# A LoRA feed-forward kernel: order of the second wave of tile products, waits per chunk ahead of gate, and the last step's transfers

## The chip, the cores and the metric

The kernel runs on one core of a Trainium2 chip, in one launch. The metric is the device time in microseconds. In a profile the engines are PE (TensorE; PEld are its weight loads, which overlap its products), DVE (VectorE), ACT (ScalarE), POOL (GpSimd) and SP (SyncE, which here only issues DMAs). ACT issues DMAs too.

## The reference, cut to what matters

There are 128 sequences of 32 tokens with 512 features, so 4096 tokens. Each sequence b has an adapter id for layer 0 (ids0, 16 adapters) and one for layer 1 (ids1, 64 adapters), each of rank 16.

```python
def lora_add(base, inp, A, B):          # A, B: the sequence's own adapter
    t = einsum('bri,bni->bnr', A[ids0], inp)
    return base + einsum('bor,bnr->bno', B[ids0], t) * 0.5
gate = lora_add(x @ W_gate.T, x, A_gate, B_gate)        # 512 -> 1376
up   = lora_add(x @ W_up.T,   x, A_up,   B_up)
act  = silu(gate) * up
down = lora_add(act @ W_down.T, act, A_down, B_down)    # 1376 -> 512
x1   = x + down @ sign(weight0).T + bias0
c    = einsum('bnr,bor->bno', einsum('bni,bri->bnr', x1, B1[ids1]), A1[ids1])
out  = x1 + c @ (W1 + 2 * sum_n w_n B_n A_n).T + bias1
```

The kernel folds the two square layers into the weights and into tables of rows per adapter in a prologue (sign(weight0) into W_down and B_down, the W1 sum into A1), so each token tile needs gate, up, down and a few small products of rank 16.

## The kernel before, in words

A step g handles 128 tokens, that is four sequences of 32 tokens; there are 32 steps. The first three and the last are written out, and steps 3 to 30 are a loop on each engine. The features of gate and up are cut in three chunks, 0 (352 wide), 1 and 2 (512 wide each), which have their own accumulator banks (`GU_BANK`). Full-precision weights are held as a rounded part and a remainder, so that each product is three rounded ones (`THREE`).

TensorE's step (`step` of the tensor block) is: gate and up of chunks 0, 1 and 2, each 12 products; in the middle of up of chunk 1 a small section (`small`) of narrow products, which gives t, the rank-16 values of the adapters, for this step's gate and up, the previous step's down and, two steps back, layer 1; then the tile session; and last down of the previous step (33 products, `down`). Before `small` it waits (`small_ready`) for the adapters' rows, the three landed chunks of act and the turned x1.

The tile session uses the array as 16 tiles of 32x32: a row group per kind of adapter rows (0 gate, 1 up, 2 layer 1, 3 down) and a column group per sequence b. A product there is in fp32 and shows as two passes, each with a load. The first wave (`first_rows`) has four products per sequence, in the order layer 1 (512 wide), down (512 wide), gate and up of chunk 0 (352 wide). The second wave (`second_rows`) has four per sequence, each 512 wide: row groups 0 and 1 for chunk 1, and row groups 2 and 3, which hold a copy of the same t, for chunk 2. It goes sequence by sequence, row groups 0 to 3 in each. In step 0 the first wave has only row groups 0 and 1, in step 1 row groups 3, 0 and 1.

After the session ACT takes silu of each chunk (L439), DVE multiplies it with up (`gated`, L591; it counts `act_done`) and turns it in blocks of 32 (L595). The turned chunk is sent from SBUF to SBUF by four DMAs (`send_act`), chunks 0 and 1 from ACT's queue and chunk 2 from SP's. Then ACT and DVE split the landed chunk into the two rounded parts for down (L428, L573). Gate of the next step writes the banks that `gated` reads, so it waits for `act_done`: once, ahead of chunk 0, for all three chunks.

SP issues its DMAs in order, in each step: xT and adapter rows of the next step, layer 1's rows (`load_b1`) and x of the previous step (`load_x`), the store of two steps back, sb rows (`load_sbd`, four DMAs), chunk 2, c rows (`load_c`, four DMAs) and the next step's B rows. After the last step, `finish` issues layer 1's rows again (`b1_end`), the last c rows, the last x and two stores. POOL adds bias0 to x when it has landed (L393); DVE then adds the down result (L668 in `finish`). On TensorE `finish` ends with a chain: turn x1 through PSUM (L949), small products for layer 1 (L833), scale and turn on DVE, last rows (L861), last add (L677), store. `keep_busy` (L920) puts products without use into its gaps.

Of the kernel before, what the change touches and what calls it, by code (L numbers as in the profile page):

```python
# [16 lines left out]
GB = P // SEQ  # L17
KC = H // P
CHUNKS = [(1024, 352), (0, 512), (512, 512)]
# [5 lines left out]
NC = len(CHUNKS)  # L25
# [11 lines left out]
PAIR = CHUNKS[0][1] + CHUNKS[1][1]  # L37
ROW = 3 * 512
LINE = 512
GU_BANK = [(4, 5), (0, 1), (2, 3)]  # L40
# [36 lines left out]
def build_adaln_ffn(nc, xT, x, wgu, signT, wd, bd, btab, atab, la, lbw, w1T, a1, b1tab, b1end,  # L77
                    bias, ids, consts, sb_table, c_table, out):
    ctx = ExitStack()
    with ctx:  # L80
# [4 lines left out]
        def place(name, shape, dtype, at=None, line=LINE):  # L85
            n = 4 * int(np.prod(shape[1:]))
            n = (n + line - 1) // line * line
            if at is None:
                at = cursor
            t = nc.alloc_sbuf_tensor_at(name, shape, dtype, offset=at[0])  # L90
            at[0] += n
            return t
# [15 lines left out]
        lhs_sb = place("lhs_sb", [P, P], f32)  # L108
        lhs2_sb = place("lhs2_sb", [P, P], f32)
        loop_at = [cursor[0]]  # L110
        b_rows = place("b_rows", [P, GB, PAIR], f32)
# [54 lines left out]
        def bank(name):  # L166
            return ctx.enter_context(nc.psum_tensor(name, [P, 512], f32))

        gu_ps = [bank(f"gu{n}_ps") for n in range(6)]
# [6 lines left out]
        def sem(name):  # L176
            return ctx.enter_context(nc.semaphore(name))
# [7 lines left out]
        S = {n: sem("pro_" + n) for n in names}  # L185
# [11 lines left out]
        L = {n: sem(n) for n in names}  # L197
# [4 lines left out]
        def after(engine, semaphore, count):  # L202

            if not isinstance(count, int) or count > 0:
                engine.wait_ge(semaphore, count)
# [4 lines left out]
        def first(g):  # L210

            return isinstance(g, int) and g == 0

        def last(g):

            return isinstance(g, int) and g == G - 1
# [13 lines left out]
        def act_in(c):  # L230

            return L[("act_in0", "act_in1", "act_in2")[c]]

        def group(r):

            return slice(r * QUAD, (r + 1) * QUAD)

        def even_rows(r0, r1):

            return slice(r0 * QUAD, r1 * QUAD, 2)  # L240

        def tokens(b):

            return slice(b * SEQ, (b + 1) * SEQ)

        def send(engine, to, tile, w, signal, quarters):
            for q in quarters:
                engine.dma_start(to[:, q * w // 4:(q + 1) * w // 4], tile[q * QUAD:(q + 1) * QUAD, 0:w]
                                 ).then_inc(signal, 16)

        def send_act(engine, g, c, quarters=range(4)):
            engine.wait_ge(L["act_turned"], g * NC + c + 1)
            send(engine, landed[c], act_sb[c], TURN_W[c], act_in(c), quarters)
# [12 lines left out]
        def _(sp):  # L266
# [26 lines left out]
            def row_of(ids, g, b, count):  # L293
                return nc.values_load(idx_feat[0:1, ids, bass.ds(g * GB + b, 1)], engines=[mybir.EngineType.SP],  # L294
                                      min_val=0, max_val=(count - 1) * P,
                                      skip_runtime_bounds_check_because="the ids are clamped on the chip")

            def load_a(g):
                for b in range(GB):
                    at = row_of(0, g, b, R0)  # L300
                    sp.dma_start(a_raw[:, b, :], atab[bass.ds(at, P), :]).then_inc(L["a_in"], 16)
# [8 lines left out]
            def load_b1(g):  # L310
                if last(g + 1 if isinstance(g, int) else g):
                    sp.wait_ge(L["small_mm"], g + 2)
                for b in range(GB):
                    at = row_of(1, g, b, R1)
                    sp.dma_start(b1_raw[:, b, :], b1tab[bass.ds(at, P), :]).then_inc(L["b1_in"], 16)

            def load_sbd(g):
                if isinstance(g, int) and g == 1:
                    sp.wait_ge(L["first_mm"], g + 1)
                for b in range(GB):  # L320
                    at = row_of(0, g, b, R0)
                    sp.dma_start(cs_rows[even_rows(3, 4), b, :], sb_view[bass.ds(at, P), :].rearrange("(r e) w -> r (e w)", e=8)  # L322
                                 ).then_inc(L["sbd_in"], 16)

            def load_c(g, to=2, signal=L["c_in"]):
                for b in range(GB):
                    at = row_of(1, g, b, R1)
                    sp.dma_start(cs_rows[even_rows(to, to + 1), b, :], c_view[bass.ds(at, P), :].rearrange("(r e) w -> r (e w)", e=8)  # L328
                                 ).then_inc(signal, 16)
# [6 lines left out]
            def load_xT(g):  # L336
                sp.wait_ge(L["ad_moved"], g)
                sp.dma_start(xT_raw[:], xT[bass.ds(g * P, P), :].rearrange("p (k t) -> p k t", k=KC)
                             ).then_inc(L["xT_in"], 16)

            def load_x(g):
                if last(g):
                    sp.wait_ge(L["x1_done"], g)
                sp.dma_start(x_in[:], x[bass.ds(g * P, P), :]).then_inc(L["x_in"], 16)

            def store(g):
                sp.wait_ge(L["out_done"], g + 1)
                sp.dma_start(out[bass.ds(g * P, P), :], out_sb[:]).then_inc(L["stored"], 16)

            def step(g, prev, pp, nxt):  # L350
                if nxt is not None:
                    load_xT(nxt)
                    load_a(nxt)
                if prev is not None:
                    load_b1(prev)
                    load_x(prev)
                if pp is not None:
                    store(pp)
                load_sbd(g)
                send_act(sp, g, 2)  # L360
                if prev is not None:
                    load_c(prev)
                if nxt is not None:
                    load_b(nxt)

            def finish(g):
                for b in range(GB):
                    at = row_of(1, g, b, R1)
                    sp.dma_start(b1_end[:, b, 0:KC * RANK], b1end[bass.ds(at, P), :]).then_inc(E["b1_in"], 16)
                load_c(g, 1, E["c_in"])  # L370
                load_x(g)
                store(g - 1)
                sp.wait_ge(L["out_done"], g + 1)
                sp.dma_start(out[g * P:(g + 1) * P, :], x1_turn[:]).then_inc(L["stored"], 16)
                sp.wait_ge(L["stored"], 16 * G)
# [7 lines left out]
            with sp.Fori(3, G - 1) as g:  # L383
                step(g, g - 1, g - 2, g + 1)
            step(G - 1, G - 2, G - 3, None)
            finish(G - 1)


# [37 lines left out]
        def _(act):  # L426
# [42 lines left out]
            def step(g, prev, pp, nxt):  # L469
                if prev is None:  # L470
                    split_up(2, range(KC))
                move_ad(g)
                copy_lhs(g)
                if nxt is not None:
                    split_xT(nxt)
                for c in range(NC):
                    silu(g, c)
                send_act(act, g, 0)
                send_act(act, g, 1)
                split_actT(g, 0)  # L480
                split_actT(g, 1)
                if prev is not None:
                    send_x1(act, prev)
                split_actT(g, 2)
# [279 lines left out]
        def _(pe):  # L764
# [8 lines left out]

            def gate(g, c, pieces=range(KC)):
                f, w = CHUNKS[c]
                if 0 in pieces and c == 0:
                    if first(g):
                        pe.wait_ge(S["wg_lo"], KC)
                    pe.wait_ge(L["xT_lo"], g + 1)
                    after(pe, L["act_done"], g * NC)  # L780
                product(gu_ps[GU_BANK[c][0]][:, 0:w], [(xT_sb[:, k, a, :], wg_sb[:, b, k, f:f + w])
                                                       for k in pieces for a, b in THREE], None,
                        start=0 in pieces, stop=KC - 1 in pieces)
# [103 lines left out]
                last.then_inc(L["first_mm"], 1)  # L887

            def second_rows():
                for b in range(GB):  # L890
                    for r in range(4):
                        c, u = 1 + r // 2, r % 2
                        lhs = lhs_sb if c == 1 else lhs2_sb
                        last = nc.tensor.matmul(gu_ps[GU_BANK[c][u]][tokens(b), :], lhs[group(r), tokens(b)],  # L894
                                                b_rows[group(r), b, CHUNKS[0][1]:PAIR], start=False, stop=True,
                                                skip_group_check=True)
                last.then_inc(L["second_mm"], 1)

            def step(g, prev, pp):
# [197 lines left out]
```

## Time and profile before

| what | value |
|---|---|
| median of 3 runs | 929.75 us (928.69 to 931.73) |
| profiled execution | 930.34 us |
| its span | 928.5 us |
| PE busy | 911.3 us (98%), 10518 products |
| PEld busy | 724.4 us (78%) |
| DVE busy | 413.7 us (45%) |
| ACT busy | 201.3 us (22%) |
| POOL busy | 105.0 us (11%) |
| mean granted clock of TensorE | 0.995 |

The span runs from the first to the last instruction, and all times in rows count from its start. The loop steps are those from about 124 to 880 us. Ends of products are modelled, so a busy PE needn't be PE at its peak; starts are recorded.

### The profile page before, as it was taken

Reading aid. Unit: us, or ns where it says so; the run is one execution under the profiler, and the core shown is the slowest. Engines: PE = TensorE matmul, PEld = TensorE weight load, DVE = VectorE, ACT = ScalarE, POOL = GpSimd, SP = SyncE. Lnnn points to the kernel's source line nnn. Section 1 sums busy time; section 2 is a strip of 40 time slices with the busy share of each in tenths; the row PEclk is TensorE's granted clock in tenths of the full one; section 3 lists DMA queues with packets and bytes.
Section 4 is the critical chain, followed back from the end, with each engine's and each line's share of the span. In section 5 each row is a group of like instructions: output and inputs, shape, how many; then the busy total and the mean of one; then the engine's idle time right before and its main releaser. Section 6 shows DMA issues by size and latency. Waiting matters only on the chain.

```text
span 928.5 us, 27750 instructions
## 1 busy us (share of the span) xinstructions
PE 911.3 (98%) x10518; PEld 724.4 (78%) x10518; DVE 413.7 (45%) x1021; ACT 201.3 (22%) x349; POOL 105.0 (11%) x81
## 2 busy tenths in 40 slices
PE   8998999999999999999999999999999999999996
PEld 5887777777887777778877777788777777887764
DVE  5753344444344444443444444434444444344442
ACT  5742211212112112121121121211211212112110
POOL 0210111010111110101111101011111010111111
PEclk9999999999999999999999999999999999999998
DMA  9924455554554455545544555555444544554432
GB/s 339 411 84 135 111 134 138 148 138 133 145 142 134 130 141 146 139 137 140 142 134 131 140 146 139 133 144 142 133 131 140 146 139 131 145 142 134 132 96 60
DMA packets 146838, 134.69 MB, mean 145 GB/s; under 512 B 53248, under 2 KB 118528, under 8 KB 146688
## 3 DMA queue, kind: packets, MB, share of 16 engines
q1 hardware_dynamic: 91152, 108.42, 40.4%
q10 hardware_dynamic: 54720, 22.83, 9.6%
q0 software_dynamic: 944, 3.15, 0.9%
q8 instruction: 14, 0.23, 0.1%
q14 instruction: 8, 0.07, 0.0%
HBM read 92.11 MB, written 11.01 MB: 111 GB/s over the span
## 4 chain that ended last, share of the span: by engine, by line
PE 94%; SPq 2%; DMA 1%; issue 1%; DVE 1%; POOL 0%; ACT 0%; DVEq 0%
PE gu_ps L768 54%; PE y_ps L803 25%; PE gu_ps L894 4%; PE out_ps L823 3%; PE out_ps L861 2%; PE out_ps L812 1%; PE y_ps L768 1%; PE out_ps L768 1%; PE out_ps L833 1%; PE gu_ps L885 1%; DMA a_raw<-in_a 1%; SPq L328 1%; SPq L294 0%; PE gu_ps L920 0%; SPq L322 0%
## 5 line engine op out<-in xcount | busy, mean ns | idle before, releaser
L768 PE MATMUL gu_ps<-wu_sb,xT_sb 128*128 128x512 f32 (+1 forms) x1152 | 260.8, 371 | 0.0
L768 PE MATMUL gu_ps<-wg_sb,xT_sb 128*128 128x512 f32 (+1 forms) x1152 | 251.8, 367 | 2.8 <-DVE act_sb L591 2.8
L803 PE MATMUL y_ps<-down_sb,actT_sb 128*128 128x512 f32 x1023 | 241.1, 393 | 0.0
L803 PEld LDWEIGHTS y_ps<-down_sb,actT_sb 128*128 128x128 f32 x1023 | 189.6, 188 | 64.4 <-issue 26.0
L768 PEld LDWEIGHTS gu_ps<-wg_sb,xT_sb 128*128 128x128 f32 x1152 | 206.8, 188 | 33.9 <-issue 3.7
L768 PEld LDWEIGHTS gu_ps<-wu_sb,xT_sb 128*128 128x128 f32 x1152 | 204.4, 188 | 28.9
L573 DVE TENSOR_TENSOR actT_sb<-landed,actT_sb 128x512 fp32r<-128x512 f32 (+1 forms) x96 | 60.7, 633 | 205.1 <-ACT actT_sb L428 205.1
L428 ACT CAST actT_sb<-landed 128x512 fp32r<-128x512 f32 (+1 forms) x96 | 56.1, 585 | 313.0 <-issue 277.4
L393 POOL TENSOR_TENSOR x_in<-x_in,bias_sb 128x512 f32<-128x512 f32 x32 | 41.3, 1292 | 589.0 <-DMA x_in<-in_x 589.0
L614 DVE STREAM_TRANSPOSE lhs_sb<-t_own 32x32 f32<-32x32 f32 x512 | 103.9, 203 | 7.7
L573 DVE TENSOR_TENSOR xT_sb<-xT_raw,xT_sb 128x512 fp32r<-128x512 f32 x32 | 22.1, 691 | 126.8 <-ACT xT_sb L428 126.8
L397 POOL TENSOR_TENSOR x_sb<-x_sb,bias_sb 128x512 f32<-128x512 f32 x31 | 51.3, 1655 | 177.3 <-DVE x_turn L626 177.3
L595 DVE STREAM_TRANSPOSE act_sb<-act_sb 128x512 f32<-128x512 f32 (+1 forms) x96 | 64.1, 668 | 3.3
L605 DVE TENSOR_TENSOR t_own<-out_ps,const_sb 128x64 f32<-128x64 f32 (+3 forms) x35 | 7.7, 219 | 124.9 <-PE out_ps L833 117.9
L591 DVE TENSOR_TENSOR act_sb<-act_sb,gu_ps 128x512 f32<-128x512 f32 (+1 forms) x96 | 58.1, 605 | 0.4 <-ACT act_sb L439 0.3
L439 ACT ACTIVATE act_sb<-gu_ps 128x512 f32<-128x512 f32 (+1 forms) x96 | 49.6, 552 | 39.7 <-PE gu_ps L885 22.9
L428 ACT COPY ad_raw<-a_raw 128x704 f32<-128x704 f32 x32 | 25.0, 782 | 146.1 <-PE out_ps L833 137.2
L894 PE MATMUL gu_ps<-b_rows,lhs_sb 32*32 32x512 f32 x1024 | 55.3, 597 | 0.0
L428 ACT CAST xT_sb<-xT_raw 128x512 fp32r<-128x512 f32 x32 | 19.8, 617 | 96.4 <-PE gu_ps L768 96.4
L861 PE MATMUL out_ps<-cs_rows,lhs_sb 32*32 32x512 f32 x256 | 35.7, 600 | 0.0
L865 PE MATMUL y_ps<-cs_rows,lhs_sb 32*32 32x512 f32 x248 | 34.7, 600 | 0.0
L894 PEld LDWEIGHTS gu_ps<-b_rows,lhs_sb 32*32 32x32 f32 x1024 | 18.7, 103 | 19.8 <-issue 16.0
(135 smaller groups left out, 498.9 us busy)
## 6 DMA issues: line engine op xcount, KB each, us to landing
b_rows<-in_btab SPq DMA_DIRECT2D x128, 216.0 KB
a_raw<-in_atab SPq DMA_DIRECT2D x128, 152.0 KB, 2.3
xT_raw<-in_xT SPq DMA_DIRECT2D x32, 256.0 KB, 2.6
landed<-act_sb ACTq DMA_DIRECT2D x128, 64.0 KB, 2.2
landed<-act_sb SPq DMA_DIRECT2D x128, 64.0 KB, 2.1
x_in<-in_x SPq DMA_DIRECT2D x32, 256.0 KB, 2.8
x_landed<-x_turn ACTq DMA_DIRECT2D x124, 64.0 KB, 2.2
out_x<-out_sb SPq DMA_DIRECT2D x31, 256.0 KB, 3.0
```

The lines of the kernel that those rows point to most:

```text
L393: nc.gpsimd.tensor_tensor(x_in[:], x_in[:], bias_sb[:, 0, :], ALU.add).then_inc(L["x_biased"], 1)
L397: nc.gpsimd.tensor_tensor(x1_sb[:], x1_sb[:], bias_sb[:, 1, :], ALU.add).then_inc(L["x1_biased"], 1)
L428: return nc.scalar.copy(o, i)
L439: nc.scalar.activation(act_sb[c][:, 0:w], gu_ps[GU_BANK[c][0]][:, 0:w], ACT.Silu).then_inc(L["silu_done"], 1)
L573: return nc.vector.tensor_tensor(o, whole, hi(high), ALU.subtract)
L591: nc.vector.tensor_tensor(a, a, gu_ps[GU_BANK[c][1]][:, 0:w], ALU.mult).then_inc(L["act_done"], 1)
L595: nc.vector.transpose(act_sb[c][:], act_sb[c][:]).then_inc(L["act_turned"], 1)
L614: turned = nc.vector.transpose(lhs_sb[group(group_of[r]), tokens(b)], wide[tokens(b), :])
L768: last = nc.tensor.matmul(o, w, m, start=start and n == 0, stop=stop and n == len(terms) - 1, skip_group_check=not check)
L803: last = nc.tensor.matmul(to[:], actT_sb[:, ACTT_SLOT[c] + n, a, :], down_sb[:, blk, b, :], start=begin and (c, n) == (0, 0) and (a, b) == ...
L861: return nc.tensor.matmul(out_ps[tokens(b), :], lhs_sb[group(r), tokens(b)], cs_rows[group(r), b, :], start=True, stop=True, skip_group_ch ...
L894: last = nc.tensor.matmul(gu_ps[GU_BANK[c][u]][tokens(b), :], lhs[group(r), tokens(b)], b_rows[group(r), b, CHUNKS[0][1]:PAIR], start=Fals ...
```

## The change

In TensorE's `gate` the single wait for all three gated chunks becomes a wait ahead of each chunk, for that chunk alone. In `second_rows` the order of the 16 products becomes: for each sequence row groups 2 and 3, then for each sequence row groups 0 and 1. In the last step SP sends chunk 1, ahead of the sb rows, and ACT sends chunks 0 and 2. In `finish` the load of x is issued first, ahead of layer 1's rows and the last c rows.

```diff
@@ SP, step
+                if last(g):
+                    send_act(sp, g, 1)
                 load_sbd(g)
-                send_act(sp, g, 2)
+                if not last(g):
+                    send_act(sp, g, 2)
@@ SP, finish
             def finish(g):
+                load_x(g)
                 for b in range(GB):
                     at = row_of(1, g, b, R1)
                     sp.dma_start(b1_end[:, b, 0:KC * RANK], b1end[bass.ds(at, P), :]).then_inc(E["b1_in"], 16)
                 load_c(g, 1, E["c_in"])
-                load_x(g)
@@ ACT, step
                 send_act(act, g, 0)
-                send_act(act, g, 1)
+                send_act(act, g, 2 if last(g) else 1)
@@ TensorE, gate
-                if 0 in pieces and c == 0:
-                    if first(g):
-                        pe.wait_ge(S["wg_lo"], KC)
-                    pe.wait_ge(L["xT_lo"], g + 1)
-                    after(pe, L["act_done"], g * NC)
+                if 0 in pieces:
+                    if c == 0:
+                        if first(g):
+                            pe.wait_ge(S["wg_lo"], KC)
+                        pe.wait_ge(L["xT_lo"], g + 1)
+                    if not first(g):
+                        pe.wait_ge(L["act_done"], g * NC - NC + c + 1)
@@ TensorE, second_rows
-                for b in range(GB):
-                    for r in range(4):
+                for b, r in [(b, r) for rows in ((2, 3), (0, 1)) for b in range(GB) for r in rows]:
...
```

## Rows read from the trace of the kernel before

**Rows 1.** The page's chain that ended last, by engine.
```profile
PE 94%; SPq 2%; DMA 1%; issue 1%; DVE 1%; POOL 0%; ACT 0%; DVEq 0%
```

**Rows 2.** The page's groups by line: busy, mean ns | idle before, releaser.
```profile
L768 PE MATMUL gu_ps<-wg_sb,xT_sb 128*128 128x512 f32 (+1 forms) x1152 | 251.8, 367 | 2.8 <-DVE act_sb L591 2.8
L803 PE MATMUL y_ps<-down_sb,actT_sb 128*128 128x512 f32 x1023 | 241.1, 393 | 0.0
```

**Rows 3.** Timeline, TensorE, step 1: start us, us, what, count [idle before].
```profile
77.68 2.17 PE L768 MATMUL gu_ps<-wg_sb,xT_sb 128*128 128x352 f32 x12 [2.82 <-DVE act_sb L591]
...
84.35 1.52 PE L768 MATMUL gu_ps<-wu_sb,xT_sb 128*128 128x512 f32 x6
```

**Rows 4.** Timeline, TensorE, after the last step.
```profile
902.71 5.05 PE L803 MATMUL gu_ps<-down_sb,actT_sb 128*128 128x512 f32 x21 [1.11 <-DVE actT_sb L573]
...
912.57 0.61 PE L865 MATMUL gu_ps<-cs_rows,lhs_sb 32*32 32x512 f32 x4
...
918.96 1.11 PE L949 MATMUL gu_ps<-const_sb,act_sb 128*128 128x128 f32 x4 [5.09 <-DVE act_sb L668]
...
924.27 1.06 PE L861 MATMUL out_ps<-cs_rows,lhs_sb 32*32 32x512 f32 x8
```

**Rows 5.** Timeline, DVE, last step and after.
```profile
895.28 0.71 DVE L595 STREAM_TRANSPOSE act_sb<-act_sb 128x512 f32<-128x512 f32 x1
...
918.48 0.75 DVE L668 TENSOR_TENSOR act_sb<-x_in,gu_ps 128x256 f32<-128x256 f32 x2 [6.75 <-POOL x_in L393]
```

**Rows 6.** Timeline, DVE, end of step 0: gating of chunks 0 and 2.
```profile
74.34 0.52 DVE L591 TENSOR_TENSOR act_sb<-act_sb,gu_ps 128x352 f32<-128x352 f32 x1
...
76.88 0.65 DVE L591 TENSOR_TENSOR act_sb<-act_sb,gu_ps 128x512 f32<-128x512 f32 x1
```

**Rows 7.** Timeline, SP's queue, step 0: chunk 2 is sent.
```profile
78.31 2.70 SPq L248 DMA_DIRECT2D landed<-act_sb  x4
```

**Rows 8.** DMA issues: count, KB each, median us from issue to landing.
```profile
landed<-act_sb SPq DMA_DIRECT2D x128, 64.0 KB, 2.1
```

**Rows 9.** Timeline, a loop session: TensorE's first wave, then its loads.
```profile
413.54 0.61 PE L861 MATMUL out_ps<-cs_rows,lhs_sb 32*32 32x512 f32 x1
...
413.99 0.59 PE L861 MATMUL out_ps<-cs_rows,lhs_sb 32*32 32x512 f32 x1
...
414.18 0.10 PEld L894 LDWEIGHTS gu_ps<-b_rows,lhs_sb 32*32 32x32 f32 x1 [0.20 <-issue]
414.61 0.36 PEld L894 LDWEIGHTS gu_ps<-b_rows,lhs_sb 32*32 32x32 f32 x30 [0.33 <-issue]
```

**Rows 10.** Timeline, sessions of steps 1 and 0: second passes and later loads.
```profile
94.44 0.65 PE L865 MATMUL y_ps<-cs_rows,lhs_sb 32*32 32x512 f32 x4
...
95.06 0.30 PEld L894 LDWEIGHTS gu_ps<-b_rows,lhs_sb 32*32 32x32 f32 x22
...
73.23 0.50 PE L885 MATMUL gu_ps<-b_rows,lhs_sb 32*32 32x352 f32 x8
...
73.72 0.23 PEld L894 LDWEIGHTS gu_ps<-b_rows,lhs_sb 32*32 32x32 f32 x14
```

**Rows 11.** Timeline, SP's queue: step 30 (first row), and after step 31.
```profile
867.87 3.92 SPq L322 DMA_DIRECT2D cs_rows<-sb_table  x4
...
906.41 3.17 SPq L369 DMA_DIRECT2D a_raw<-in_b1end  x4
910.07 4.07 SPq L328 DMA_DIRECT2D cs_rows<-c_table  x4
914.19 0.57 SPq L344 DMA_DIRECT2D x_in<-in_x  x1
```

**Rows 12.** Timeline, ACT's queue: chunks 0 and 1 sent, steps 30 and 31.
```profile
867.58 5.38 ACTq L248 DMA_DIRECT2D landed<-act_sb  x8
...
894.69 6.76 ACTq L248 DMA_DIRECT2D landed<-act_sb  x8
```

**Rows 13.** Windows: stretch, its us, busy us (count) of PE, PEld, DVE, ACT, POOL, PEclk, DMA share, GB/s.
```profile
916.40:923.00 6.60, 4.04 (x42) 2.95 (x43) 2.69 (x9) 0.37 (x1) 2.53 (x2) 0.50 0.12 47
```

More of the change, by code:

```diff
@@ L889, in second_rows @@
             def second_rows():
-                for b in range(GB):
-                    for r in range(4):
[L892 to L896, printed above, removed]
+                for b, r in [(b, r) for rows in ((2, 3), (0, 1)) for b in range(GB) for r in rows]:
+                    c, u = 1 + r // 2, r % 2
+                    lhs = lhs_sb if c == 1 else lhs2_sb
+                    last = nc.tensor.matmul(gu_ps[GU_BANK[c][u]][tokens(b), :], lhs[group(r), tokens(b)],
+                                            b_rows[group(r), b, CHUNKS[0][1]:PAIR], start=False, stop=True,
+                                            skip_group_check=True)
                 last.then_inc(L["second_mm"], 1)
```

## The prediction

> **What bounds the kernel now.** I read the page's engine shares and chain of waits first: TensorE is busy 98% of the span and is 94% of the chain [rows 1]. So only idle time of TensorE, or a change in how long its own instructions run, can move the time. The groups by line then say where it idles: in 1152 gate products only 2.8 us, in one place, behind L591, and in the 1023 down products not at all [rows 2]. The timeline shows the holes that the change can reach: the start of step 1, 2.82 us before 77.68 [rows 3]; and in the last step 1.11 us before 902.71 and 5.09 us before 918.96 [rows 4], the latter behind adds that start at 918.48 and were released by POOL, which had waited for x [rows 5].
>
> **Part 1, waits per chunk: step 1.** Today step 1's first gate waits until all three chunks of step 0 are gated, 76.88 + 0.65 = 77.53 [rows 6], and starts 0.15 later. Afterwards it needs only the first chunk, gated at 74.34 + 0.52 = 74.86, so it starts at 75.01: 2.67 us earlier. The split of xT stands ahead of that gating on DVE, so it is done. The session before has its loads done at 73.95 [rows 10]; its last passes start by 74.3 and stream 0.43. The second chunk's gate comes 24 products later, near 78.9; by then even the third chunk (77.53) is gated, so neither new wait is felt. What is late next is the small section: ahead of the second piece of up stands the wait for the landed third chunk of step 0. SP issues it from 78.31 for 2.70 us [rows 7], the last of the four near 80.4, and 2.1 us to landing [rows 8] make it 82.5. Nothing in the change moves that. The piece begins today after three of the six products that start at 84.35, each 0.23: at 85.04 [rows 3]. 2.67 earlier would be 82.37; the wait lets its first load go at about 82.75 and its matmul at 82.95. 0.6 us is given back. **Gain 2.05** (bounds: 2.67 if the landing doesn't hold it, 1.4 if it lands 0.6 later). SP, ACT and DVE follow TensorE from there, and no product of the loop waits for anything else, so the shift is carried to the end.
>
> **Part 1 in the loop.** Two waits per step are new there, 56 in all, each for a count made in a register, on chunks gated before the step's first gate began. Behind each stand all of TensorE's later products. But the wait they copy stands in 31 steps and cost idle time in one [rows 2], and at least six products of 0.23 us run ahead of either new one while it is looked at. I take 0. The other end is the shortest pause of the loads in a session, 0.20 [rows 9]: 56 x 0.20 = 11 us, if nothing ran ahead.
>
> **Part 2, the order of the second wave.** No product is added. The first wave has 16 products of two passes each, one per 32x32 tile; a tile's second pass starts 0.45 after its first (413.54, 413.99). Then one product of the second wave goes (load at 414.18), and nothing more until 414.61, when the other 15 go in one burst, 30 loads in 0.36 us [rows 9]. The session's end hangs on that 414.61. What releases it? The very first product's second pass ends at 413.99 + 0.59 = 414.58, 0.03 before. In step 1, whose first wave has 12 products, the first one's second pass ends at 94.44 + 0.59 = 95.03 and the burst is at 95.06. In step 0, with 8 of 352 columns (eight within 0.50 us, so 0.45 each), it ends at 73.23 + 0.45 = 73.68 and the burst is at 73.72 [rows 10]. Counted in program order 17 products had been let in each time (16 + 1, 12 + 5, 8 + 9): the eighteenth goes when the first is finished. By that reading the order within the second wave doesn't matter: the first product stays the same, 17 are let in whichever they are, and by 414.6 the tiles of the other 15 are free. The one now in place 17, in row group 2, would start at 414.42 and its second pass at 414.85, ahead of the last. **Gain 0.** Ends: 0.40 us per step slower (rival a), or the 0.43 from 414.18 to 414.61 faster, were the pause to vanish.
>
> The Trainium skill speaks against this part: "TensorE: Matmul & The Clock Gate", section "The mechanism" (packing small matmuls), has matmuls start and finish strictly in program order. By that rule the new lead, whose tile is taken longest, holds back all that follow it. The trace doesn't agree: in step 0 the first loads of product 18 and on go at 73.72, while product 17's second pass can't have begun before 73.95: its tile was taken by a second pass from 73.23 at the earliest (0.43 x 352/512 = 0.30), and its own first pass takes 0.43.
>
> **Part 3, the last step.** SP today: sb rows and third chunk to 901.8, c rows, b1 rows 906.41 to 909.6, c rows 910.07 to 914.14, then x at 914.19 [rows 11]; 4.3 us later, landed and biased, it lets the adds into x1 start at 918.48 [rows 5], though TensorE's last down rows ended at 912.57 + 0.61 = 913.18 [rows 4]. The new SP order, with today's durations: second chunk from its turning, 895.28 + 0.71 = 896.0 [rows 5], to 898.65; sb rows after 0.45, at 3.92 as in the step before, to 903.0; c rows at 4.0 to 907.0; x at 907.05, biased by 911.35; b1 rows to 911.2, landed by 913; c rows to 915.1 or 915.6. The last of these is issued 0.5 earlier and lands some 2.1 after that, if it takes what SP's chunks take [rows 8]: 916.7 to 917.2, or 1.1 later if the sendings are as slow as here (below). I take 917.3.
> TensorE's own part up to 913.18 stays. ACT sends eight pieces as before (chunks 0 and 2 for 0 and 1), its later casts stay behind the turning of x1, and the sb rows (landed 904.6) and the first c rows (908.6) are wanted after 912. So the adds start at 913.25 instead of 918.48, and down's end binds: 5.2 us.
> From these adds to the last rows it takes 924.27 - 918.48 = 5.79 us today. In that stretch the granted clock is 0.50, the lower level of 1.2 GHz [rows 13], and it fell after TensorE had stood idle from 913.87. Without the hole I expect the upper level: ten filler products at 0.24 instead of some 0.4 us save about 1.5, which makes 4.4 and puts the rows at 917.65. They also need the last c rows, 917.3, and one filler product behind that wait. I take 917.85 against 924.27. **Gain 6.4** (bounds: 5.2 if the clock falls all the same, 7.7 if also the 1.11 us hole goes). That hole: ACT's eight sendings took 6.76 us, against 5.38 one step before [rows 12], and its cast of the first chunk comes after them. If that was chance, it goes; the swap of chunks doesn't cause it, and I count nothing.
>
> **The sum.** 2.05 + 0 + 6.4 = 8.45 us. The profiled execution took 930.34 us, 1.84 more than its span of 928.5; so 921.9 in its terms. The median of the runs shown, 929.75, is 0.6 below it: **921.3 us**.
>
> **Rivals.**
> (a) *The lead holds the queue* (the other side). The second wave's lead waits for its tile, and everything behind it in order waits too. It would start at 414.42 instead of 414.18: 0.24 per step, 7.2 us in 30 steps, so 921.3 + 7.2 = 928.5, no change. If it is held to the earlier product's modelled end, 414.58, it is 0.40 per step and 12 us: 933.3, slower. It decides from 8.45 / 30 = 0.28 us per step. For it: one product alone between 414.18 and 414.61. Against: steps 0 and 1, as above. 9% at the first price, 4% at the second.
> (b) *The tail gives less:* the c rows, now behind x and b1 rows, land late, or the clock falls. It then brings 3.5 to 5.2: about 923.5. For it: SP has no pause from 896 to 915. 15%.
> (c) *The second wave gains:* the pause before 414.61 depends in part on what stands in place 17; 0.2 per step, 6 us: 915.3. Nothing in step 0 or 1 speaks for it. 4%.
> (d) *The new waits show,* 0.05 to 0.1 us each: 924 to 927. Against: [rows 2]. 4%.
> (e) *It doesn't do what it says:* the landing holds step 1 where it is, and something else than x holds the adds: 929.7. Against: [rows 5, 7]. 2%.
> The forecast has 62%.
>
> **How the numbers follow.** 0.3%, 2.8 us, is about what a measurement of this kernel can tell from no change. The forecast, (b), (c) and most of (d) are faster: 0.84. The first price of (a) and (e): the same, 0.11; the second price of (a) and the rest: slower, 0.05. The range ends at 918.5 (all upper bounds, 10.4 us, give 919.4, and a little of (c)) and at 926.5 (it takes in (b) and most of (d), and leaves (a) out). The forecast's own range is 919.4 to 923.3.
>
> **What would show it.** Step 1's first gate near 75.0, and from the small section on a shift of about 2 us. In each loop session the burst of 30 loads still 1.07 us after the first product; (a) would make it 1.3 or more. In the last step no idle time over 1 us on TensorE after 903, a clock of 1.0 to the last rows, the adds released by TensorE, and the last rows within 0.5 us of the last c rows' landing. The forecast is wrong if a loop step gets longer or shorter by over 0.1 us.

## The result, and the profile after

| what | before | after |
|---|---|---|
| median of the runs | 930.08 us (928.69 to 931.73, 4 runs) | 921.18 us (920.11 to 922.48, 4 runs) |
| ratio | | 0.990, 95% interval 0.988 to 0.993 |
| profiled execution, its span | 930.34, 928.5 us | 921.35, 919.5 us |
| mean granted clock | 0.995 | 1.000 |

The forecast was 921.3 us. Below, "the session" of a step is the start of its first tile product, the one recorded start that every kernel here has in every step. The prologue ended 0.79 us earlier in this execution of the changed kernel (session 0 at 72.12, before at 72.91), so stretches are compared and not clock times.

| stretch, us | before | after | gain |
|---|---|---|---|
| session 0 to step 1's first gate product | 4.77 | 2.09 | 2.68 |
| session 0 to session 1 | 21.08 | 19.10 | 1.98 |
| session 0 to session 2 | 49.15 | 47.52 | 1.63 |
| a loop step, mean of 27 | 26.515 | 26.524 | -0.01 |
| session 31 to the first add into x1 | 26.94 | 21.11 | 5.83 |
| that add to the last rows | 5.79 | 4.49 | 1.30 |

The page's chain by engine answers to [rows 1]; DVE and SP's queue have nearly left it:

```profile
PE 96%; DMA 1%; DVE 1%; ACTq 1%; issue 1%; SPq 0%; ACT 0%
```

Its groups by line (busy us, mean ns | idle before, releaser) answer to [rows 2]. Of the 2.8 us ahead of gate 0.1 is left, and a new 0.3 stands ahead of up, behind a landed chunk:

```profile
L771 PE MATMUL gu_ps<-wu_sb,xT_sb 128*128 128x512 f32 (+1 forms) x1152 | 261.1, 371 | 0.3 <-DMA landed<-act_sb 0.3
L771 PE MATMUL gu_ps<-wg_sb,xT_sb 128*128 128x512 f32 (+1 forms) x1152 | 251.9, 367 | 0.1
L808 PE MATMUL y_ps<-down_sb,actT_sb 128*128 128x512 f32 x1023 | 241.1, 393 | 0.0
```

TensorE in step 1 (start us, us, what, count [idle before]), which answers to [rows 3]: the first gate at 74.21, and the second piece of up, which starts 0.30 after the products ahead of it end, because it waits for the landed chunk:

```profile
74.21 2.16 PE L771 MATMUL gu_ps<-wg_sb,xT_sb 128*128 128x352 f32 x12
...
80.87 0.84 PE L771 MATMUL gu_ps<-wu_sb,xT_sb 128*128 128x512 f32 x3
82.01 0.93 PE L771 MATMUL gu_ps<-wu_sb,xT_sb 128*128 128x512 f32 x3 [0.30 <-DMA landed<-act_sb]
```

The same loop session as in [rows 9], TensorE's products:

```profile
411.31 0.61 PE L866 MATMUL out_ps<-cs_rows,lhs_sb 32*32 32x512 f32 x1
...
411.77 0.59 PE L866 MATMUL out_ps<-cs_rows,lhs_sb 32*32 32x512 f32 x1
...
412.19 1.47 PE L898 MATMUL gu_ps<-b_rows,lhs_sb 32*32 32x512 f32 x32
413.59 2.11 PE L808 MATMUL y_ps<-down_sb,actT_sb 128*128 128x512 f32 x8
```

And of the kernel before, the same two last groups:

```profile
414.18 1.71 PE L894 MATMUL gu_ps<-b_rows,lhs_sb 32*32 32x512 f32 x32
415.82 1.43 PE L803 MATMUL y_ps<-down_sb,actT_sb 128*128 128x512 f32 x5
```

The lead of the second wave starts 0.88 after the session's start instead of 0.64, for its tile is busy until then. The end stays: down follows at 2.28 in both (413.59 - 411.31, 415.82 - 413.54). By the single records the other 15 products start from 1.08 after the session's start, in both.

TensorE after the last step answers to [rows 4]:

```profile
900.25 5.05 PE L808 MATMUL gu_ps<-down_sb,actT_sb 128*128 128x512 f32 x21 [0.52 <-DVE actT_sb L576]
...
911.26 0.77 PE L953 MATMUL gu_ps<-const_sb,act_sb 128*128 128x128 f32 x4
...
913.35 1.99 PE L924 MATMUL gu_ps<-wg_sb 128*128 128x512 f32 x7
915.27 1.06 PE L866 MATMUL out_ps<-cs_rows,lhs_sb 32*32 32x512 f32 x8
```

DVE's adds into x1 are released by TensorE, no longer by POOL [rows 5]:

```profile
910.78 0.75 DVE L671 TENSOR_TENSOR act_sb<-x_in,gu_ps 128x256 f32<-128x256 f32 x2 [1.51 <-PE gu_ps L870]
```

SP's queue in the new order (answers to [rows 11]): chunk 1, sb rows, c rows, x, layer 1's rows, the last c rows:

```profile
894.15 2.56 SPq L248 DMA_DIRECT2D landed<-act_sb  x4
897.22 3.65 SPq L322 DMA_DIRECT2D cs_rows<-sb_table  x4
901.35 3.45 SPq L328 DMA_DIRECT2D cs_rows<-c_table  x4
904.85 0.57 SPq L344 DMA_DIRECT2D x_in<-in_x  x1
905.93 3.41 SPq L373 DMA_DIRECT2D a_raw<-in_b1end  x4
909.82 3.50 SPq L328 DMA_DIRECT2D cs_rows<-c_table  x4
```

And the window over the end (columns as in [rows 13]); the clock is 1.00 there, not 0.50:

```profile
911.00:916.40 5.40, 5.28 (x56) 2.59 (x54) 2.47 (x10) 0.37 (x1) 1.28 (x1) 1.00 0.24 73
```

### The profile page after: what moved, and what is told of

It reads as the page before. It is cut to its first block, busy times and chain, and to the rows that moved or that the text cites. A ratio compares the mean times of both kernels' runs of the same rounds, so it can differ in the third digit from the quotient of the medians.

```text
span 919.5 us, 27778 instructions
## 1 busy us (share of the span) xinstructions
PE 910.7 (99%) x10518; PEld 723.2 (79%) x10518; DVE 413.6 (45%) x1021; ACT 201.1 (22%) x349; POOL 105.0 (11%) x81
## 4 chain that ended last, share of the span: by engine, by line
PE 96%; DMA 1%; DVE 1%; ACTq 1%; issue 1%; SPq 0%; ACT 0%
PE gu_ps L771 54%; PE y_ps L808 25%; PE gu_ps L898 4%; PE out_ps L828 3%; PE out_ps L866 2%; PE y_ps L771 1%; PE out_ps L817 1%; PE out_ps L771 1%; PE out_ps L838 1%; PE gu_ps L890 1%; PE gu_ps L808 1%; DMA weff_raw<-in_w1T 1%; ACTq L248 1%; PE gu_ps L924 0%; DMA landed<-act_sb 0%
## 5 line engine op out<-in xcount | busy, mean ns | idle before, releaser
L898 PE MATMUL gu_ps<-b_rows,lhs_sb 32*32 32x512 f32 x1024 | 48.1, 597 | 0.0
```

## The experiments

Ratios are to the kernel before, measured beside each on the same chip, with 95% intervals. Kernels whose name says one part alone are the kernel before with that part.

### The parts one by one

Part 1 alone: the waits per chunk, as in the diff of the change (TensorE, `gate`).

> The kernel before, with the waits per chunk ahead of gate alone. My theory: step 1's first gate starts 2.1 us after the first product of step 0's session instead of 4.8, 0.5 to 0.6 us is given back where the small section waits for the landed third chunk, and the loop is as before: 2.1 us faster in the profile, some 928. Rival: the new waits show in the loop, 0.05 to 0.1 us each in 56 places, and eat the gain or more: 929 to 934, with loop steps over 26.6 us.

Measured: 926.89 us (10 runs; before 930.4), ratio 0.9964 (0.9952 to 0.9976), so 3.3 us with 2.2 to 4.5 as interval. The profile has the first gate at session 0 + 2.09 and the small section at + 10.71, as in the changed kernel (2.09 and 10.75).

Part 2 alone: the order of the second wave.

> The kernel before, with the second wave in the new order alone. My theory (17 products are let in, the eighteenth goes when the first is finished): no change, 930, each loop session's burst of loads still 1.07 us after its first product and down's first load 2.28 after it. Rival: products go strictly in order, so the lead holds up the others, 0.24 to 0.40 us per step: 937 to 942. Rival: the wide row groups are served earlier and the session gets shorter by up to 0.2 us: 924.

Measured: 931.67 us (12 runs), ratio 1.0009 (0.9998 to 1.0020). A loop step takes 26.503 us (before 26.515), and from the session's start to down it is 2.278 us in the median of the loop steps, in this kernel, before and after alike. By the loop steps part 2 brings nothing and costs nothing: rivals (a) and (c) are out. The timed runs allow it between 0.2 us faster and 1.9 slower, and their medians are 1.3 us apart. A difference of that size can come of a lost clock, and this kernel's profile has one.

After the pause ahead of step 1's first gate the products ran at half speed. These are TensorE's groups there, and the window over the first twelve:

```profile
76.49 3.86 PE L768 MATMUL gu_ps<-wg_sb,xT_sb 128*128 128x352 f32 x12 [2.82 <-DVE act_sb L591]
80.15 3.21 PE L768 MATMUL gu_ps<-wu_sb,xT_sb 128*128 128x352 f32 x12
```

```profile
76.50:79.90 3.40, 3.40 (x12) 3.40 (x13) 0.59 (x1) 0.35 (x1) 0.00 (x0) 0.50 0.50 127
```

The pause is the same 2.82 us as in [rows 3], where the twelve took 2.17 us at a clock of 1.00. Here the granted clock is 0.50, the lower level of 1.2 GHz, and step 1's small section comes 2.78 us later (15.67 after session 0 in place of 12.89).

Part 3 cut in two. First the load of x ahead of layer 1's rows and the last c rows, alone:

> The kernel before, with the last x load moved ahead of layer 1's rows and the last c rows alone. My theory: this is the whole of the tail's gain. The adds start near 913.3 instead of 918.5, the clock stays at its upper level, and the last rows come 4.1 us after the adds (scale and turn on DVE bind, the c rows have landed before): 6.9 us faster, 923. Rival: the sendings of the last step are a part of it; then this kernel gains only 4 to 5 us.

Measured: 924.07 us (6 runs), ratio 0.9933 (0.9916 to 0.9950), 6.2 us with 4.7 to 7.8 as interval. The adds come 21.27 after session 31 and the last rows 4.39 later: 25.66 in all, where the changed kernel has 25.60. So by the traces the moved load is the whole of the end's gain, as expected, and the sendings are no part of it. Its step 1 had the drop of the clock too: the first twelve products took 3.64 us, the window over them shows 0.54, and the small section came at 14.43.

Then the swap of chunks 1 and 2 between ACT and SP, alone:

> The kernel before, with chunks 1 and 2 of the last step sent by the other queue each, chunk 1 ahead of the sb rows, alone. My theory: the last x load still binds, and SP, which now waits for the turned second chunk before it goes on, issues it 0.8 us later: 0.8 us slower, 930.8, though TensorE's hole ahead of the last down gets 0.5 us shorter. Rival: the swap starts down earlier and that is carried to the end: 0.6 to 1.1 us faster.

Measured: 931.60 us (12 runs), ratio 1.0014 (1.0003 to 1.0025): 1.3 us slower, with 0.3 to 2.3 as interval. The adds start 27.90 after session 31, the latest of all profiles (25.45 to 26.94 in the other five in which x is loaded last). SP's next DMA behind the store now waits for the turned chunk 1, 4.48 after session 31, where before the sb rows went at 2.95, and x, the last in the queue, is issued 23.68 after session 31, against 21.19 to 22.65 in those five. With x moved ahead the swap no longer delays the adds, which then wait for TensorE: the changed kernel has them 0.16 earlier than the kernel with the load of x alone (21.11 and 21.27). But SP issues the last c rows 1.1 us later there (the last ends 23.64 and not 22.51 after session 31), so that the end comes to wait for them.

### Is it the clock? Products without use in the two pauses

In the kernel before, the stretch ahead of the turning of x1 is filled:

```diff
@@ TensorE, finish
-                keep_busy(2)
+                keep_busy(22)
```

> The kernel before, with 22 instead of 2 products without use ahead of the turning of x1 in the end chain, so that TensorE doesn't stand idle while x is awaited; the x load stays where it is. My theory: the late x costs twice, 5.2 us for the adds that start late and 1.4 us because the clock has fallen by then. Filled, the adds still start 26 to 27 us after the last session's first product, but the last rows come 4.3 us after them instead of 5.8, at a granted clock of 1.0: some 1.4 us faster, 929. Rival: the end chain is bound by DVE, ACT and the semaphores, the clock doesn't matter, and it stays 5.8 us: 930.4.

Measured: 929.43 us (12 runs), ratio 0.9996 (0.9984 to 1.0009). The profile shows what was meant: the clock is 1.00 over the whole end, and from the adds to the last rows it is 4.59 us. This is the window from the fillers to the last rows:

```profile
910.80:921.70 10.90, 10.85 (x93) 6.92 (x92) 2.76 (x9) 0.37 (x1) 2.56 (x2) 1.00 0.18 56
```

The other profiles with the pause unfilled have 5.79 to 6.68 there. So the clock explains the shorter end in the trace. The timed gain, 0.4 us with -0.8 to 1.5 as interval, is smaller than the 1.2 to 2.1 us of the traces, although the 4.59 holds what the fillers cost (the turning starts 0.86 after the adds instead of 0.48). The profiled execution is not typical here: it is the fastest of the twelve, and only it and one other, 926.72 and 926.94 us, have a mean granted clock of 1.000. The other ten took 928.29 to 933.09 us at 0.994 to 0.998, so they lost the clock somewhere, and where is not on record. The trace shows what the clock costs in this stretch; that filling the pause makes the kernel faster is not shown by the times.

In step 1 the same: twelve products into a bank that is free, ahead of the first gate of the kernel before.

```diff
@@ TensorE, step, ahead of gate(g, 0), in step 1 alone
+                    for _ in range(12):
+                        nc.tensor.matmul(y_ps[:], wg_sb[:, 0, 0, 0:P], wg_sb[:, 0, 0, 0:512], start=True, stop=True)
```

> The kernel before, with 12 products without use (into a bank that is free then) in TensorE's pause ahead of step 1's first gate; that gate still waits for all three chunks. The runs of single parts showed that in some executions the clock falls to 0.50 behind this pause (in two of four profiles with the pause, gate's 12 products took 3.4 and 3.2 us instead of 1.9), which the profile of the kernel before had not shown. My theory: the waits per chunk gained 3.3 us where 2.1 was worked out because they take that risk away too. Then filling the pause, which moves no wait, gives the rest: 1.0 to 1.3 us faster in the median, 929.2, with a spread over the runs of under 2.5 us instead of 5.6. Rival: the rest of the gain has another cause, and filling the pause changes nothing: 930.4, spread as before.

Measured: 928.93 us (11 runs; before 930.06), ratio 0.9993 (0.9983 to 1.0004). The medians are 1.1 us apart, the interval of the ratio gives -0.4 to 1.6. The profile has the twelve gate products at 2.16 us. Of the five profiles with an unfilled pause (before, the order, the load of x, the swap, the filled end) two lost the clock there, 2.78 and 1.54 us: 0.9 us in the mean. That agrees with what was timed but is not shown by it. The spread over the runs, expected to fall below 2.5 us, is 3.7 (4.1 in the kernel before beside it): that sign failed. The mean granted clocks of the timed runs say a little more. In 9 of the 10 runs of the waits alone the clock was 0.995 or 0.996, but in 3 of the 27 of the kernel before beside them, most of which had 0.994; with the pause filled it was that high in 6 of 11 runs, against 5 of 23. Over all 61 such runs of the kernel before those with 0.995 or 0.996 took 929.1 us in the mean and those with 0.994 took 930.6. So both come with less lost clock, and that is worth time; whether it was lost in step 1 or at the end the runs don't tell.

### The hole in the last step's down products

[rows 4] has 1.11 us ahead of 902.71; the changed kernel has 0.52. Is that chance? First the changed kernel once more.

> The changed kernel itself once more, beside the others on the same chip: 921.2, between 920.1 and 922.5. A second profile of it shows whether the hole before the second run of down products (0.52 us) and the longer sendings (6.17 us) come in every execution, as the instruction fetch would have it, or by chance.

Measured: 921.99 us (4 runs; before 930.44), ratio 0.9903 (0.9877 to 0.9929). The hole is 0.51 us and ACT's eight sendings take 6.16 us; in the first profile 0.52 and 6.17. So the 0.52 is not chance, but half a microsecond of the 1.11 is. Five other kernels send the last step's chunks as before. Four of them (the waits, the order, the load of x, the filled end) have in their profiles holes of 0.67 to 0.69 and sendings of 6.32 to 6.34 us. In each a transfer of 16 KB in the queue "instruction" runs for 0.95 to 0.97 us while ACT sends. In the profiled execution of the kernel before that transfer took 1.99 us, the sendings 6.76 and the hole 1.11. The swap of chunks itself takes some 0.16 off the hole. Then the changed kernel with 32 waits that are already satisfied, which shift TensorE's instructions against the code's blocks:

```diff
@@ TensorE, last step, ahead of gate
+                    for _ in range(32):
+                        pe.wait_ge(S["idle_set"], 1)
```

> The changed kernel with 32 waits that are already satisfied placed on TensorE ahead of the last step's first gate, so that the same 16 KB instruction fetch falls some microseconds earlier against the work. What is told apart: the hole on TensorE ahead of the second run of down products in the last step (1.11 us before, 0.52 after; chance in the prediction). Theory: it is not chance; the fetch (892 to 894 after) falls among ACT's eight sendings of chunks and holds them up, 6.17 us in place of 5.38. Moved ahead of them it leaves them at 5.4 and the hole falls from 0.52 to 0.1 or less. It may cost up to 1 us where it stands: 32 waits by some 0.03 to 0.06 us each, partly beside queued products. Rival: the eight sendings are slow because SP sends at the same time; then they stay at 6.2 and the hole at 0.5. Time between 919.5 and 922 either way; the trace decides.

Measured: 921.25 us (1 run). The packet of 16 KB in the queue "instruction" starts at 893.64 in the changed kernel, 3.97 after session 31's start, and at 891.56 here, 2.44 after it. It ends at 892.75, and the next comes after 900. ACT's sendings in the changed kernel:

```profile
892.82 6.17 ACTq L248 DMA_DIRECT2D landed<-act_sb  x8
```

and with the fetch moved ahead of all but the first of them, ACT and then TensorE:

```profile
892.26 5.21 ACTq L248 DMA_DIRECT2D landed<-act_sb  x8
```

```profile
899.01 5.28 PE L808 MATMUL gu_ps<-down_sb,actT_sb 128*128 128x512 f32 x21
```

The sendings are 0.96 us shorter and the hole is gone, while SP still sends beside ACT; the rival, that SP's sending slows ACT's, is out. The fifth kernel, the one with step 1's pause filled, shows the same without being made for it: its twelve products shift TensorE's code too, the packet starts 2.28 after session 31, ACT's sendings take 5.40 us, and there is no hole. The time is no better: x is now what the adds wait for (they start 21.30 after session 31), and the last rows come 25.76 after it (25.60 in the changed kernel).

### Kernels beyond the change

First wave of the changed kernel with its narrow products (352 columns) first, the eight wide ones behind:

```diff
@@ TensorE, first_rows
                 for b in range(GB):
-                    if pp is not None:
-                        out_rows(b)
-                    if prev is not None:
-                        down_rows(b)
                     for u in range(2):
...
+                for b in range(GB):
+                    if pp is not None:
+                        last = out_rows(b)
+                    if prev is not None:
+                        last = down_rows(b)
```

> The changed kernel, with the first wave reordered: the eight products of 352 columns first, then the eight of 512. My theory (17 products are let in; each later one goes when the one 17 places ahead is finished): the pause ends when the first narrow product is finished, 0.81 us after the session's start instead of 1.07, products 18 to 25 go then, and 26 to 32 wait for the first wide ones, to 1.13. The last second pass starts at 1.68 instead of 1.76 and down's first load comes 2.20 after the start instead of 2.28: 0.08 us in each of 31 steps, 2.5 us faster than the changed kernel, 918.7. Rival: program order holds the queue, each product behind the one before it; then the first wave's order changes nothing or costs up to 0.1 us per step: 921 to 924.

Measured: 918.90 us (4 runs), ratio 0.9886 (0.9868 to 0.9904). A loop step takes 26.436 us, 0.088 less, and from session to down it is 2.198 instead of 2.278. Its loop session, TensorE's loads:

```profile
410.00 0.15 PEld L886 LDWEIGHTS gu_ps<-b_rows,lhs_sb 32*32 32x32 f32 x12 [0.35 <-issue]
...
410.51 0.10 PEld L899 LDWEIGHTS gu_ps<-b_rows,lhs_sb 32*32 32x32 f32 x1 [0.28 <-issue]
410.80 0.55 PEld L899 LDWEIGHTS gu_ps<-b_rows,lhs_sb 32*32 32x32 f32 x31 [0.19 <-issue]
```

The first product now has 352 columns; its second pass starts at 410.32 and, taking 0.45, ends at 410.77. The burst comes at 410.80, 0.80 after the session's start and not 1.07. This is the rule that the prediction read from [rows 9, 10], tried by changing which product is first. The single loads bear it out at a second place. Eight products go in from 410.80 to 410.92, number 18 to 25, and the other seven only from 411.12, the row below (each product has two loads). Number 26 is the seventeenth behind number 9, the first of the wide ones, whose second pass starts at 410.50 and, at 0.59, ends at 411.09. That pause was in the expectation, at 1.13 after the start; it is at 1.12.

```profile
411.12 0.23 PEld L899 LDWEIGHTS gu_ps<-b_rows,lhs_sb 32*32 32x32 f32 x14
```

The wait for the landed chunks in step 1 one piece of up later:

```diff
@@ TensorE, step, in step 1 alone
-                small_ready(g, prev, pp)
                 up(g, 1, range(1, 2))
+                small_ready(g, prev, pp)
```

> The changed kernel, with step 1's wait for the landed chunks put behind the second piece of up instead of ahead of it. My theory: the pause of 0.3 to 0.7 us ahead of that piece is this wait, which lets go when the third chunk of step 0 has landed; three products run in its place, and the small section starts 0.5 us earlier after step 0's session (10.2 instead of 10.75). Rival: the small section is held by something else there, the pause moves behind the piece, and it starts at 10.7 as before.

Measured: 920.0 us (1 run). The small section is at session 0 + 10.21 (10.75 in the changed kernel): the 0.5 us that the landing took back is regained.

These two and one filler less together:

```diff
@@ TensorE, finish, besides the two diffs above
                 pe.wait_ge(E["c_in"], 16 * GB)
-                keep_busy(1)
```

> The changed kernel with three things more: in the first wave the eight narrow products (352 columns) go first; in step 1 the wait for the landed chunks stands one piece of up later; and the filler product behind the wait for the last c rows is gone. Expected against the changed kernel: 0.08 us per loop step, 2.3 us in all, as the narrow-first kernel alone gave; 0.5 us in step 1; 0.25 to 0.5 us at the end, where the last c rows and the filler behind them are what the last rows wait for. Sum 3.0 to 3.3: 918.0, between 917.3 and 919. Rival: the end is bound by SP's queue, which does not move with TensorE when TensorE comes earlier; then the last rows keep waiting for the c rows by up to 0.5 us more, and 918.5 is the time. If the clock falls in the end without the filler, about 919.

Measured: 919.08 us (6 runs, 916.28 to 920.43; before 930.44), ratio 0.9876 (0.9854 to 0.9898). That is at the upper end of the expected 917.3 to 919, and just beyond it. The profile has the shortest span of all, 915.4 us, with each term in it: 26.445 per loop step, the small section at 10.21. The last rows still wait for the c rows, as the rival had it:

```profile
911.11 1.06 PE L866 MATMUL out_ps<-cs_rows,lhs_sb 32*32 32x512 f32 x8 [0.38 <-DMA cs_rows<-c_table]
```

It beats the changed kernel by 2.9 us in the medians of the same chip (921.99), but is not told apart from the kernel with the narrow products first alone. Its runs spread over 4 us: the three fastest (916.28 to 918.46) have a mean clock of 0.999 or 1.000, the three others (919.70 to 920.43) 0.995 to 0.998. Where the clock was lost in those is open.

## Why the prediction was right

**The forecast held, 921.3 against 921.18 us, and so did the mechanism of each part. That it came so near is luck in part: two of its terms were off and balanced.** In the profiles the 9.0 us of span are 0.79 of prologue, with which the change has nothing to do, 1.1 for part 1 where 2.05 was worked out, and 7.1 for part 3 where 6.4 was.

**Step 1.** First gate 2.67 earlier: measured 2.68. Neither new wait was felt, and the landing gave back 0.54 (2.68 less the 2.14 gained at the small section) for the 0.6 that was worked out. The term of 2.05 is 1.98 at session 1. From there the text said that the shift is carried to the end; in the profiles 1.63 of it was left at session 2 and 1.1 at session 31 (1.87 less the prologue's 0.79). Some 0.35 was lost in step 2, where TensorE pauses 1.91 us in the small section and paused 1.55 before; 0.25 in the 27 loop steps, 0.009 each, which is within what the kernels with the same first wave differ by (26.503 to 26.524); and 0.3 from session 30 to 31, which took 27.51 instead of 27.21. That last stretch is between 26.60 and 28.13 over all kernels, and 26.92 in the second profile of the changed one, so of this 0.3 nothing can be said.

**The size of part 1 in the timed runs.** Alone it gained 3.3 us, more than 2.05. The interval, 2.2 to 4.5, begins just above that. The weak step of the prediction is that it let the profile of before stand for all its executions: it shows step 1's pause with no loss of clock, and two of four later profiles with the same pause show the loss. The stretch from session 0 to the small section is 12.88 to 15.67 in the five profiles with the pause, 13.76 in the mean, and 10.71 to 10.77 in the five with the new waits at their place: 3.0 us. The part takes away a pause, and with it a chance of the lower level. That this makes up the whole difference is argued and not shown: filling the pause alone gave nothing that stands clear of noise.

**Part 1 in the loop.** No price was taken for 56 waits; a loop step of the waits alone is 26.514 us against 26.515. Rival (d) is out.

**Part 2.** Right, and by its reason: the lead starts when its tile comes free, the others when the first product of the session is finished. One sign that was named failed in its letter: the burst of loads isn't 1.07 after the start but 0.89, since the lead's own second load, 0.19 ahead of the rest, is in the same row. The 0.40 of rival (a) did not come, and its 0.24 came for the lead alone: nothing behind was let in later. Nor do the passes go in strict program order, as the prediction had read from step 0: in the changed kernel's session the lead's second pass starts at 412.62, after the first passes of the 15 products behind it, which start from 412.39 on.

**Part 3.** 6.4 was worked out, and the two profiles have 7.13 (5.83 + 1.30). The adds were put at down's end and are released by it. Most of the difference is the 1.11 us hole, of which the text counted nothing: 0.59 of it went, 0.43 because the profiled execution of before had an unusually long one (0.67 to 0.69 in four others) and 0.16 by the swap. The text's "the swap of chunks doesn't cause it" was right for the most part. The clock stayed up as expected. From the adds to the last rows the sum had 4.6 us, 4.4 and the wait for the c rows (917.85 - 913.25), and 4.49 were measured.

The late x was worse than usual in that execution as well: the adds started 26.94 after session 31, and 25.45 to 26.03 in the four other profiles with x last and the chunks as before. Against the three of those without fillers (31.83, 32.61 and 32.13 from session 31 to the last rows) the changed kernel's 25.60 gains 6.2 to 7.0, and the load of x alone was timed at 6.2.

The last c rows were not late: issued by 913.32, they landed at 914.73, 1.4 after the last issue and not 2.1, and the rows went 25.60 after session 31, with 26.3 worked out. Rival (b) is out, but closely: the end is bound by these c rows and one filler behind them, and in the second profile of the same kernel they cost 0.98 us of idle time, and the last rows came 26.71 after session 31. One of layer 1's rows ahead of them took SP 1.43 us to issue there and 0.58 in the first profile, beside a transfer in the queue "instruction".

**What gains.** The load of x gives 6.2 of the 8.9 us and the waits 3.3 (their ratios multiplied are 0.990, that of the whole change), the order nothing. The swap alone costs 1.3; beside the moved load it gives 0.16 at the adds and puts the c rows in the way behind them, which comes to nothing in one profile (25.60 against 25.66) and to a loss in the other (26.71).

## What to carry to other kernels

Where products of different width share an array in waves, look for the product that is first in program order: it, and not the tile that frees last, set when the eighteenth went here, and putting the narrow ones first gave 0.09 us per step. On a queue that issues in order, put first what the longest chain behind it needs; one moved load was worth two thirds of this change. And a pause of TensorE has two prices, itself and the clock after it, and one profile shows only one draw of the second.

## What the runs showed that was not expected

- **The same pause, with and without the lower clock.** Step 1's 2.82 us was followed by 0.50 or 0.54 in two profiles of five. In step 2's small section the changed kernel pauses 1.91 us in one profile and 1.88 in the other; only in the second do the products behind it run at half speed, and session 2 is 1.5 us later. The two windows from 112.60 on, first profile and second:

```profile
112.60:115.20 2.60, 2.60 (x15) 2.17 (x12) 2.30 (x12) 0.78 (x1) 0.00 (x0) 1.00 0.27 61
```

```profile
112.60:116.00 3.40, 3.40 (x13) 2.71 (x12) 3.04 (x15) 0.78 (x1) 0.00 (x0) 0.58 0.34 88
```

- **A fetch of 16 KB of instructions holds up DMAs that other engines issue.** In the changed kernel it runs from 893.64 to 894.60, and the sending that ACT was at took 1.58 us and ended at 894.98; before it ran from 894.82 to 896.81 and ACT's and SP's ended at 897.19: each 0.38 after the fetch's end. Moving TensorE's code by 32 waits moved the fetch and shortened the sendings. Not every sending pays: the first of ACT's eight took the usual 0.55 us although it ran beside the fetch before and in the shifted kernel. The loop steps fetch nothing; the written-out steps do. The Trainium skill ("Runtime: NRT & Kernel Launch", section "Instruction fetch mechanics") has an engine's instructions refilled in blocks of 16 KiB by DMA while it works on the block before, and takes that as hidden by the rate at which instructions are issued. The size agrees with the packets here (16 KB). That it is hidden does not hold for the other engines here, for with the fetch elsewhere ACT's sendings are 0.96 us shorter.
- **A product is let in by the end of the seventeenth before it.** Sessions with 512 and with 352 columns in the first product have their burst at 1.07 and 0.80 after it; a new order of the second wave left the 1.07 as it was. With the narrow products first number 26 goes at 1.12, when number 9 ends at 1.09. Only these two places, the eighteenth and the twenty-sixth, were seen to wait so.
